# Expert tiles of a routed layer: bias rows of all experts kept in both weight buffers and picked by one-hot rows, the two additions of a tile issued together, eight output tiles

## The chip, the core and the metric

The kernel runs on one core of one Trainium2 chip. The metric is the device time of one execution in microseconds (us). Before the change it is 929.73 us, the median of 3 runs (926.41 to 929.73).

## What is computed

A four-layer network on 32 images and 32 texts (96 tokens of width 192 per batch): patch embedding with a binary activation, attention with 12 heads, a soft mixture of 64 slots, causal attention with rotary positions, and at the end a routed mixture of 8 experts. The change lies in the last one. Cut to what matters:

```
gate_logits = x_flat @ Wr                       # 3072 tokens, 8 experts
topw, topi = jax.lax.top_k(gate_logits, 2); topw = jax.nn.softmax(topw, axis=-1)
combine = zeros((T, 8)).at[arange(T)[:, None], topi].add(topw)
h = jax.nn.relu(jnp.einsum('td,edh->eth', x_flat, W1) + b1[:, None, :])    # 192 -> 768
y = jnp.einsum('eth,ehd->etd', h, W2) + b2[:, None, :]                     # 768 -> 192
out = jnp.einsum('te,etd->td', combine, y)                                 # added to the input
```

## The kernel before, in words

The program runs phase after phase on all engines. `route` sorts the (token, expert) pairs by expert into 31 tiles of 256 rows (`NTB`; 62 halves of 128 rows, `NTILES`), each tile with one expert. It leaves the row numbers (`g.idx`), the expert of each tile (`g.te`, and `g.te_less` in float), and in DRAM a table of the normalized tokens (`xtab`). It also splits the first bias `b1` into a high and a low part and writes both to a small DRAM table (`b1tab`, POOL, L1704 to L1711).

`expert_tiles` (L1840 to the end) then works the tiles off. Its stages are laid over each other: in step t the engines do the transposes of tile t, the first product of tile t-1, the second product of tile t-2, and bias, weight and addition of tile t-3. The order of the stages on an engine is written out by hand (`steps`, L94): steps 0 to 7 and the last ones are straight code, steps 8 to 27 are a loop of 4 steps per turn. All products run in split float32r (high and low part).

- **SP** (L1877 to L1892) loads for each tile the expert's first-layer weights into one of two buffers (`w_buf`) by four DMAs: three for the weights (L1881, L1883, L1885; 1344 KB) and one for the two bias rows from `b1tab` into rows 64 and 65 of part 3 (L1887, 6 KB). It waits until the first product of the tile two before is done. Behind the ones of tile 1 it loads the second bias for all experts (`x_b`, L1892).
- **POOL** fetches the rows of a tile by two indirect DMAs of 128 rows (L1900, into `late`) and adds the finished rows to the output by two indirect DMAs with addition (L1919). The loop over half tiles alternates: fetch of half t, addition of half t-10 (`BEHIND`). The additions of a tile wait until both additions of the tile before have landed, as two of them may hit the same output row. Behind its second fetch POOL writes the rows of ones that the bias rows are multiplied by (L1904 to L1907).
- **PE**: `first(k)`, k = 0 to 5 (L2037), five matmuls into one of three banks of PSUM; the last has 66 rows, 64 of the input's low part and the two of ones. It waits for DVE's low part of `first(k-3)`, since the bank comes free with it. `second(k)` (L2053, L2056) multiplies with the second weights, which all stay in SBUF. The transposes (L2019) stand between `second(1)` and `first(2)`.
- **ACT**: relu into the high part (L1936); `x_copy` takes the transposed input's high part (L1929) as soon as the transposes are done; `weigh` multiplies the output rows by the gate (L1943). Order in a step: relu 0, relu 1, x_copy, weigh 0, relu 2, weigh 1, relu 3 to 5.
- **DVE**: low parts of relu (L1976) and of the input (`x_rest`, L1969, L1970), the gate weights (`pick`, L1962, L1965), and `add_bias` (L1982 to L1990): it loads the expert's number from SBUF into a register (L1982, TENSOR_LOAD), waits for the second product and for `s_add` (the output tile must be free), and adds bias and product into one of four output tiles (`ys`, `NYS`; two tiles' worth). Order: add_bias 0, low parts 0 and 1, pick, x_rest, add_bias 1, low parts 2 to 5.

Of the kernel before, what the change touches and what calls it, by code (L numbers as in the profile page):

```python
# [146 lines left out]
def build(nc, A):  # L147
    with ExitStack() as ctx:
# [11 lines left out]
        g.te_less = sb("te_less", [128, NTB])  # L160
        g.te = sb("te", [128, NTB], mybir.dt.int32)
# [27 lines left out]
        with ExitStack() as lists:  # L189
# [32 lines left out]
            g.iota, g.padrow = small("iota", [128, 128]), small("padrow", [128, 2])  # L222
# [46 lines left out]
def expert_weights(nc, g, held):  # L269
# [27 lines left out]
    for i in range(NWB):  # L297
        g.w1_buf.append(halves(f"buf_{i}", [128, 4, F])[:, :, :])

# [986 lines left out]
def attention1(nc, A, g):  # L1286


    with ExitStack() as ctx:
# [8 lines left out]
        vv = sb("vv", [T, 4, D])  # L1298
        ra = sb("ra", [T, 2, 2 * D])
        rb = sb("rb", [T, 2, 2 * D])  # L1300
        qkT = sb("qkT", [HALF, 2, 4, T])
# [336 lines left out]
def route(nc, A, g):  # L1638


    with ExitStack() as ctx:  # L1641
# [26 lines left out]
        tokens = sb("tokens", [T, 2, PART, 128], F32R)  # L1668
        NL = NTILES + NTILES % 2
        occ = sb("occ", [T, 2, PART, NL], F32R)  # L1670
# [12 lines left out]
        def _(sp):  # L1683
# [16 lines left out]
            sp.wait_ge(g.s_b1r, 32)  # L1700
# [28 lines left out]
        def _(v):  # L1729
# [80 lines left out]
            v.tensor_scalar(g.te_less[:, :], tef[:, :], float(-NE), None, ALU.add)  # L1810
            v.wait_ge(s_list, 1)
# [23 lines left out]
def expert_tiles(nc, A, g):  # L1835
# [3 lines left out]
    with ExitStack() as ctx:  # L1839
# [3 lines left out]
        def sb(name, shape, dt=F32):  # L1843
# [3 lines left out]
        NYS = 4  # L1847
        BEHIND = 10
        xg, ys = carve(g.late, ([128, NX, DX], [128, NYS, D]))
        one = sb("one", [128, 256])  # L1850
        x_hi = sb("x_hi", [128, 2, 2, MT], F32R)
        x_lo = sb("x_lo", [128, 2, 2, MT], F32R)
        h_hi = sb("h_hi", [128, FC, MT], F32R)
        h_lo = sb("h_lo", [128, FC, MT], F32R)
        b2 = sb("b2", [128, NE, D])
        picked = sb("picked", [128, 2, 2])
        s_pick, s_cw = sem("pick"), sem("cw")
        (s_b2, s_mem, s_one, s_lo_v, s_sum, s_xTp, s_xh, s_xl, s_h1, s_hh, s_hl, s_y, s_ya, s_ys) = (
            sem(n) for n in ("b2", "mem", "one", "lo_v", "sum", "xTp", "xh", "xl", "h1", "hh", "hl", "y", "ya", "ys"))
# [11 lines left out]
        def _(sp):  # L1871
# [3 lines left out]
            sp.wait_ge(g.s_b1r, 32)  # L1875
            for i in range(NTB):
# [10 lines left out]
                sp.dma_start(buf[64:66, 3, :], A["b1tab"][:, bass.ds(e * F, F)]).then_inc(done, 16)  # L1887
# [7 lines left out]
        def _(pool):  # L1895
            for t in range(NTILES + BEHIND):
                if t < NTILES:
                    if t >= NX:
                        pool.wait_ge(s_cw, (t - NX) // 2 + 1)
                    pool.indirect_dma_start(out=xg[:, t % NX, :], out_offset=None, in_=A["xtab"][:, :],  # L1900
                                            in_offset=bass.IndirectOffsetOnAxis(ap=g.idx[:, t:t + 1], axis=0)
                                            ).then_inc(s_x[t % NX], 16)
                if t == 1:
                    pool.memset(one[:, :], 1.0).then_inc(s_mem, 1)  # L1904
                    pool.wait_ge(s_mem, 1)
                    for n in range(2):
                        pool.tensor_copy(x_lo[:, n, 1, :], one[:, :]).then_inc(s_one, 1)  # L1907
                        pool.wait_ge(s_one, n + 1)
                if t == NX - 1:
# [4 lines left out]
                i = t - BEHIND  # L1914
                if i >= 0:
                    pool.wait_ge(s_ys, i + 1)
                    if i >= 2:
                        pool.wait_ge(s_add, 32 * (i // 2))
                    pool.indirect_dma_start(out=A["out"][:, :],  # L1919
                                            out_offset=bass.IndirectOffsetOnAxis(ap=g.idx[:, i:i + 1], axis=0),  # L1920
                                            in_=ys[:, i % NYS, :], in_offset=None, compute_op=ALU.add).then_inc(s_add, 16)
# [3 lines left out]
        def _(act):  # L1925
            def x_copy(i, u):
                item(act, s_xTp, i)
                reused(act, s_h1, i, 2, FC)
                act.activation(x_hi[:, u % 2, :, :], b_x, ACT.Copy).then_inc(s_xh, 1)  # L1929
# [9 lines left out]
            def weigh(half):  # L1939
                def stage(i, u):  # L1940
                    act.wait_ge(s_ya, i * 2 + half + 1)
                    out = ys[:, (2 * u + half) % NYS, :]
                    act.activation(out, out, ACT.Copy, scale=g.cw[:, bass.ds(i * 2 + half, 1)]).then_inc(s_ys, 1)  # L1943
                return stage

            steps(act, NTB, [(relu(0), 1), (relu(1), 1), (x_copy, 0), (weigh(0), 3), (relu(2), 1), (weigh(1), 3),
# [3 lines left out]
        def _(v):  # L1950
# [5 lines left out]
            v.wait_ge(s_one, 2)  # L1956
# [23 lines left out]
            def add_bias(half):  # L1980
                def stage(i, u):
                    e = v.value_load(g.te[0:1, bass.ds(i, 1)], min_val=0, max_val=NE - 1)  # L1982
                    item(v, s_y, i, FC)
                    if not isinstance(i, int) or i >= 2:
                        v.wait_ge(s_add, i * 32 - 32)
                    out, bank = ys[:, (2 * u + half) % NYS, :], b_y[u % 2][half]
# [10 lines left out]
        def _(pe):  # L1997
            pe.wait_ge(s_one, 2)
# [24 lines left out]
            def first(k):  # L2023
                def stage(i, u):
                    w = g.w1_buf[u % NWB]
                    cols = slice(128 * k, 128 * k + 128)
                    if k == 0:
                        item(pe, s_xl, i)
                        if isinstance(i, int):
                            pe.wait_ge(g.s_w1[i % NWB], 64 * (i // NWB + 1))  # L2030
                        else:
                            pe.wait_ge(g.s_w1[u % NWB], (i - u) * (64 // NWB) + (64 * (u // NWB) + 64))
# [109 lines left out]
```

## Time and profile before

| | |
|---|---|
| median of 3 runs | 929.73 us |
| the profiled execution | 929.62 us |
| its span, first to last instruction | 927.8 us |
| PE busy over the span | 758.7 us (82%) |
| DVE, ACT, POOL busy | 540.8, 421.0, 354.6 us |
| expert tiles, first matmul to the span's end | from 657.5 us on |
| granted TensorE clock, mean | 0.886 |

Engines in the profile: PE is TensorE's matmuls, PEld its weight loads, DVE VectorE, ACT ScalarE, POOL GpSimd, SPq the queue of SyncE; a small q behind a name stands for that engine's sequencer. A matmul's busy time overlaps with the next one's, so PE's busy share says little; starts are what to read. Rows of the timeline give start, duration, engine, line, instruction, what it writes and reads, and in brackets the engine's idle time before it and what ended that.

### The profile page before, as it was taken

The page shows a single profiled execution, that of the slowest core. Times are in us where ns is not written, and L with a number is a line of the kernel's source. Part 1 is how long each engine was busy: PE and PEld are TensorE (multiplying, and loading weights), DVE is VectorE, ACT ScalarE, POOL GpSimd, SP SyncE. Part 2 cuts the span into 40 slices and gives each one's busy share as a digit, 9 for nine tenths or more (in the row PEclk, how much of TensorE's full clock was granted, in tenths as well). Part 3 has the DMA queues.
Part 4 walks back from the last instruction along what each step waited for, and adds up shares of the span by engine and source line. Part 5 has one row for each costly group of instructions (what it writes and reads, how often), then busy time and mean ns, then how long its engine had stood idle before and what let it go on. Part 6 is the DMA issues. An engine that isn't in the chain of part 4 may idle for free. (4 is left out here: it accounts for less than half of the span.)

```text
span 927.8 us, 23887 instructions
## 1 busy us (share of the span) xinstructions
PE 758.7 (82%) x8516; PEld 646.9 (70%) x8517; DVE 540.8 (58%) x1494; ACT 421.0 (45%) x1072; POOL 354.6 (38%) x391
## 2 busy tenths in 40 slices
PE   3689999999977766656689999926299999999992
PEld 3578888888864445434557778716299999999992
DVE  1698888787851311212467777779255555655562
ACT  3666776766642311111115777562144444444441
POOL 1433444444321000000103878410636666666654
PEclk9799999999965987787759999955599999999997
DMA  9419100000025999999347000062578888887872
GB/s 243 128 28 431 56 2 2 2 2 3 1 73 191 390 427 427 426 426 418 95 164 319 26 28 1 27 151 35 188 229 233 238 235 237 233 234 228 236 189 30
DMA packets 55133, 163.12 MB, mean 176 GB/s; under 512 B 12352, under 2 KB 30338, under 8 KB 50688
## 3 DMA queue, kind: packets, MB, share of 16 engines
q1 hardware_dynamic: 43072, 147.45, 43.1%
q0 software_dynamic: 11968, 14.41, 8.8%
q8 instruction: 62, 1.02, 0.4%
q14 instruction: 31, 0.25, 0.1%
HBM read 107.01 MB, written 12.16 MB: 128 GB/s over the span
## 5 line engine op out<-in xcount | busy, mean ns | idle before, releaser
L2037 PE MATMUL psum<-x_x_hi,w_buf 128*128 128x256 f32 x558 | 127.9, 299 | 14.1 <-DVE x_x_lo L1970 9.1
L1919 POOL DMA_INDIRECT out_h<-late,idx x62 | 98.4, 1587 | 71.4 <-DMA out_h<-late,idx 59.6
L2053 PE MATMUL psum<-w_pairs,x_h_hi 128*128 x372 | 116.1, 350 | 0.0
L1936 ACT ACTIVATE x_h_hi<-psum 128x256 fp32r<-128x256 f32 x186 | 68.5, 380 | 93.2 <-PE psum L2056 78.9
L2037 PEld LDWEIGHTS psum<-x_x_hi,w_buf 128*128 128x128 f32 x558 | 92.0, 192 | 20.5 <-DVE x_h_lo L1976 10.8
L1976 DVE SCALAR_TENSOR_TENSOR x_h_lo<-psum,x_h_hi 128x256 fp32r<-128x256 f32 x186 | 75.8, 420 | 52.3 <-ACT x_h_hi L1936 51.5
L2037 PE MATMUL psum<-x_x_lo,w_buf 128*128 128x256 f32 x372 | 97.5, 284 | 0.0
L2056 PE MATMUL psum<-w_pairs,x_h_lo 128*128 x372 | 93.2, 251 | 0.0
L1900 POOL DMA_INDIRECT late<-xtab,idx x62 | 61.2, 987 | 73.6 <-POOLq L1641 40.5
L536 POOL TENSOR_SCALAR a_u<-flat,a_mv 96x192 f32<-96x192 f32 x32 | 24.3, 758 | 133.8 <-DVE a_mv L708 133.8
L2056 PEld LDWEIGHTS psum<-w_pairs,x_h_lo 128*128 128x128 f32 x372 | 71.2, 191 | 0.0
L2037 PEld LDWEIGHTS psum<-x_x_lo,w_buf 128*128 128x128 f32 x372 | 71.1, 191 | 0.0
L2053 PEld LDWEIGHTS psum<-w_pairs,x_h_hi 128*128 128x128 f32 x372 | 70.4, 189 | 0.0
L639 ACT ACTIVATE ring<-psum 96x384 f32<-96x384 f32 x96 | 46.5, 484 | 28.2 <-PE psum L954 27.1
L1265 PE MATMUL psum<-flat,late 128*32 128x96 f32 x1152 | 35.8, 292 | 26.8 <-DMA flat<-in_slot_w 18.4
L1181 POOL MEMSET f_hid<- 96x96 f32 x1 | 0.2, 179 | 149.4 <-PE psum L1249 149.4
L1265 PEld LDWEIGHTS psum<-flat,late 128*32 128x32 f32 x1152 | 32.3, 134 | 33.6 <-DMA flat<-in_slot_w 23.2
L954 PE MATMUL psum<-ident,ring 96*96 96x96 f32 x384 | 50.4, 255 | 2.5 <-ACT ring L632 1.2
L1943 ACT ACTIVATE late<-late,cw 128x192 f32<-128x192 f32 x62 | 28.0, 452 | 51.1 <-DVE late L1990 51.1
L1207 DVE TENSOR_TENSOR m_y<-psum,m_y 128x384 f32<-128x384 f32 x8 | 7.3, 914 | 75.1 <-PE psum L1265 75.1
L1165 ACT ACTIVATE late<-late 128x512 f32<-128x512 f32 x24 | 14.7, 630 | 77.1 <-DVE late L1197 76.9
L1579 PE MATMUL psum<-late,b_xT 96*96 96x384 f32 x128 | 49.3, 510 | 0.0
(268 smaller groups left out, 1947.8 us busy)
## 6 DMA issues: line engine op xcount, KB each, us to landing
flat<-in_slot_w SPq DMA_DIRECT2D x23, 2304.0 KB, 30.3
w_buf<-w_first SPq DMA_DIRECT2D x31, 768.0 KB
ring<-in_slot_w SPq DMA_DIRECT2D x8, 2304.0 KB, 30.3
w_buf<-w_hi_a SPq DMA_DIRECT2D x31, 384.0 KB
flat<-in_moe_w SPq DMA_DIRECT2D x1, 10752.0 KB, 29.7
flat<-in_x_patches SPq DMA_DIRECT2D x4, 1536.0 KB, 14.5
w_buf<-w_first SPq DMA_DIRECT2D x31, 192.0 KB
flat<-in_slot_w SPq DMA_DIRECT2D x4, 576.0 KB, 33.8
```

Source lines behind the costliest of these rows:

```text
L639: act.activation(pT[:, r, :, :], bank_pT(b, r).rearrange("p (h t) -> p h t", t=T), ACT.Copy).then_inc(s_pTs, 1)
L954: mm = pe.transpose(bank_pT(b, r)[:, j * T:(j + 1) * T], p[:, b % 2, r * HG + j, :], g.ident[0:T, 0:T])
L1265: mm = pe.matmul(b_y[32 * quad:32 * quad + 32, 2 * r + j, :], hT[:, FC * r + k, B * c:B * (c + 1)], w2[:, c, k, half * HALF:(half + 1) * H ...
L1579: mm = pe.matmul(b_qk, xT[:, i % 2, k, :], wqkv[:, k, 0:2 * D], start=(k == 0), stop=(k == 1))
L1900: pool.indirect_dma_start(out=xg[:, t % NX, :], out_offset=None, in_=A["xtab"][:, :], in_offset=bass.IndirectOffsetOnAxis(ap=g.idx[:, t:t ...
L1919: pool.indirect_dma_start(out=A["out"][:, :], out_offset=bass.IndirectOffsetOnAxis(ap=g.idx[:, i:i + 1], axis=0), in_=ys[:, i % NYS, :], i ...
L1936: act.activation(h_hi[:, k, :], b_f[k % NF1], ACT.Relu).then_inc(s_hh, 1)
L1943: act.activation(out, out, ACT.Copy, scale=g.cw[:, bass.ds(i * 2 + half, 1)]).then_inc(s_ys, 1)
L1976: v.scalar_tensor_tensor(h_lo[:, k, :], b_f[k % NF1], 0.0, h_hi[:, k, :].bitcast(F32), ALU.max, ALU.subtract).then_inc(s_hl, 1)
L2037: mm = pe.matmul(b_f[k % NF1], w[0:rows, part, cols], x[0:rows, u % 2, c, :], start=(m == 0), stop=(m == len(terms) - 1))
L2053: pe.matmul(bank, h_hi[:, k, part], g.w_pairs[:, :, k, bass.ds(e, 1), :].rearrange("p two a d -> p two (a d)"), start=(k == 0), stop=False)
L2056: mm = pe.matmul(bank[:, 1, :], h_lo[:, k, part], g.w_pairs[:, 1, k, bass.ds(e, 1), :].rearrange("p a d -> p (a d)"), start=False, stop=(k ...
```

## The change

1. **Bias rows.** `route` writes the high and low bias rows of all 8 experts once into both weight buffers (rows 64 to 79 of part 3: four DMAs instead of two, on POOL). The DMA per tile and `b1tab` go. Instead of rows of ones, rows 64 to 79 of the input's low part hold a one in the two rows of the tile's expert: ACT writes them for each tile, ahead of the copy of the high part (16x256, from a column of ones times the one-hot column `g.te_hot`, which DVE computes once in `route`). The last matmul of `first(k)` has 80 rows instead of 66.
2. **Additions.** POOL issues both additions of tile t-5, then both fetches of tile t. Only the first of the two waits for the tile before.
3. **Output tiles.** Eight instead of four (four tiles' worth); DVE waits for the additions of the tile four before, where it waited for those of the tile two before.
4. **Memory.** `h_hi` and `h_lo` share a region (`w_work`) with tiles of the phases before, as do `x_one` and `x_picked` with `late`; the memory so freed holds the new output tiles (`x_ys`).

```diff
 (build)
+        g.te_hot = sb("te_hot", [128, NTB])
 (route, GpSimd)
             for i, row in enumerate((b1_hi, b1_lo)):
-                pool.dma_start(A["b1tab"][i:i + 1, :].rearrange("a (p f) -> (a p) f", p=128),
-                               row[:, :].bitcast(F32)).then_inc(g.s_b1r, 16)
+                for buf in g.w1_buf:
+                    to = buf[64 + NE * i:64 + NE * (i + 1), 3, :].bitcast(F32)
+                    pool.dma_start(to.rearrange("e (q f) -> e q f", q=16), row[:, :].bitcast(F32)).then_inc(g.s_b1r, 16)
 (route, VectorE)
+            v.tensor_scalar(g.te_hot[:, :], tef[:, :], padrow[:, 2:3], None, ALU.is_equal)
 (expert_tiles)
-        NYS = 4
-        BEHIND = 10
+        NYS = 8
+        BEHIND = 5
 (expert_tiles, SyncE, per tile)
-                sp.dma_start(buf[64:66, 3, :], A["b1tab"][:, bass.ds(e * F, F)]).then_inc(done, 16)
 (expert_tiles, GpSimd)
-            for t in range(NTILES + BEHIND):
...
+            def add_rows(t):
+                pool.wait_ge(s_add, 32 * t) if t else None
+                for i in (2 * t, 2 * t + 1):
+                    pool.wait_ge(s_ys, i + 1)
+                    pool.indirect_dma_start(out=A["out"][:, :],
...
+            for t in range(NTB + BEHIND):
+                if t >= BEHIND:
+                    add_rows(t - BEHIND)
+                if t < NTB:
+                    fetch(t)
 (expert_tiles, ScalarE, x_copy)
+                act.activation(x_lo[64:64 + 2 * NE, u % 2, 1, :], one[64:64 + 2 * NE, :].broadcast_to([2 * NE, MT]), ACT.Copy,
+                               scale=g.te_hot[64:64 + 2 * NE, bass.ds(i, 1)])
                 act.activation(x_hi[:, u % 2, :, :], b_x, ACT.Copy).then_inc(s_xh, 1)
 (expert_tiles, VectorE, add_bias)
-                    if not isinstance(i, int) or i >= 2:
-                        v.wait_ge(s_add, i * 32 - 32)
+                    if not isinstance(i, int) or i >= 4:
+                        v.wait_ge(s_add, i * 32 - 96)
 (expert_tiles, TensorE, first)
-                    terms = (..., (x_lo, 1, 3, 66))
+                    terms = (..., (x_lo, 1, 3, 64 + 2 * NE))
```

Where instructions move: POOL's queue at the head of `expert_tiles`, before the change (`late<-xtab` is a fetch, `out_h` an addition, `w_pairs` a part of the second weights):

```order
L1900 DMA late<-xtab,idx 128x260 x2
L1904 MEMSET x_one 128x256
L1907 CAST x_x_lo<-x_one 128x256 x2
L1900 DMA late<-xtab,idx 128x260 x2
L1913 TENSOR_TENSOR w_pairs<-flat,w_pairs 128x768 x4
L1900 DMA late<-xtab,idx 128x260 x7
L1919 DMA out_h<-late,idx 3328x192
L1900 DMA late<-xtab,idx 128x260
```

The same place after it:

```order
L1897 MEMSET late 128x1
L1903 DMA late<-xtab,idx 128x260 x4
L1924 TENSOR_TENSOR w_pairs<-flat,w_pairs 128x768 x4
L1903 DMA late<-xtab,idx 128x260 x6
L1911 DMA out_h<-late,idx 3328x192 x2
L1903 DMA late<-xtab,idx 128x260 x2
L1911 DMA out_h<-late,idx 3328x192 x2
L1903 DMA late<-xtab,idx 128x260 x2
L1911 DMA out_h<-x_ys,idx 3328x192 x2
```

The fetch that stood between the two additions of a tile now stands behind both, and the rows of ones are gone from between the fetches of tiles 0 and 1.

ACT's queue at the end of the loop over steps, before the change (two steps, from relu 0 and 1 on):

```order
L1936 ACTIVATE x_h_hi<-psum 128x256 x2
L1929 ACTIVATE x_x_hi<-psum 128x512
L1943 ACTIVATE late<-late,cw 128x192
L1936 ACTIVATE x_h_hi<-psum 128x256
L1943 ACTIVATE late<-late,cw 128x192
```

A step in the middle of the loop after it, with its register instructions:

```order
L1941 ACTIVATE w_work<-psum 128x256
L1938 REGISTER_ALU
L1940 REGISTER_ALU
L1941 ACTIVATE w_work<-psum 128x256
L87 REGISTER_ALU
L94 ISA
L1932 ISA
L1932 ACTIVATE x_x_lo<-late,te_hot 16x256
L1934 ACTIVATE x_x_hi<-psum 128x512
L1946 ISA
L1948 ISA
L1948 ACTIVATE x_ys<-x_ys,cw 128x192
```

The one-hot rows (L1932) stand between the wait for the transposes and the copy of the high part (before L1929, now L1934).

## Rows read from the trace of the kernel before

**Rows 1.** The page: the chain that ended last, by engine and line

```profile
DMA out_h<-late,idx 9%; PE psum L2037 4%; PE psum L2053 2%; POOL late L1900 2%; POOL out_h L1919 1%; PE psum L2056 1%; DMA late<-xtab,idx 1%; PE psum L2019 1%; DMA x_b<-in_moe_b 0%; SPq L1885 0%; DMA w_buf<-b1tab 0%; DVE x_h_lo L1976 0%; SPq L1881 0%; ACT late L1943 0%; SPq L1883 0%
```

**Rows 2.** Timeline, PE: transposes of tiles 3, 16, 17, 18, 29, 30

```profile
683.70 0.60 PE L2019 MATMUL psum<-ident,late 128*128 128x128 f32 x4
...
785.88 0.60 PE L2019 MATMUL psum<-ident,late 128*128 128x128 f32 x4
793.73 0.60 PE L2019 MATMUL psum<-ident,late 128*128 128x128 f32 x4
801.33 0.60 PE L2019 MATMUL psum<-ident,late 128*128 128x128 f32 x4
...
888.08 0.60 PE L2019 MATMUL psum<-ident,late 128*128 128x128 f32 x4
895.50 0.60 PE L2019 MATMUL psum<-ident,late 128*128 128x128 f32 x4
```

**Rows 3.** Timeline of step 17: ACT, DVE, and the matmul first(5)

```profile
794.45 0.60 ACT L1929 ACTIVATE x_x_hi<-psum 128x512 fp32r<-128x512 f32 x1
795.45 0.41 DVE L1970 TENSOR_TENSOR x_x_lo<-psum,x_x_hi 64x256 fp32r<-64x256 f32 x1
796.61 0.36 DVE L1987 TENSOR_TENSOR late<-psum,x_b 128x192 f32<-128x192 f32 x1 [0.75 <-DMA out_h<-late,idx]
797.75 0.50 PE L2037 MATMUL psum<-x_x_hi,w_buf 128*128 128x256 f32 x2
```

**Rows 4.** Register loads, L1982, steps 10, 17, 17: count, ns, start us

```profile
L1982 DVEq TENSOR_LOAD <-te x1: 425/425/425, 740.1 to 740.1; - x1
...
L1982 DVEq TENSOR_LOAD <-te x1: 301/301/301, 792.2 to 792.2; - x1
...
L1982 DVEq TENSOR_LOAD <-te x1: 957/957/957, 795.1 to 795.1; - x1
```

**Rows 5.** Timeline, POOL: additions and fetches at those loads

```profile
740.53 1.59 POOL L1919 DMA_INDIRECT out_h<-late,idx  x1 [0.30 <-ACT late L1943]
...
794.70 1.59 POOL L1919 DMA_INDIRECT out_h<-late,idx  x1 [0.30 <-issue]
796.60 0.98 POOL L1900 DMA_INDIRECT late<-xtab,idx  x1 [0.31 <-issue]
799.61 1.59 POOL L1919 DMA_INDIRECT out_h<-late,idx  x1 [2.02 <-DMA out_h<-late,idx]
```

**Rows 6.** Timeline, DVE: x_rest and add_bias 1 in step 16, a loop turn's first

```profile
788.15 0.41 DVE L1970 TENSOR_TENSOR x_x_lo<-psum,x_x_hi 64x256 fp32r<-64x256 f32 x1
789.01 0.36 DVE L1987 TENSOR_TENSOR late<-psum,x_b 128x192 f32<-128x192 f32 x1 [0.46 <-PE psum L2056]
```

**Rows 7.** Timeline, ACT: a weighting and the relu right behind it

```profile
876.57 0.46 ACT L1943 ACTIVATE late<-late,cw 128x192 f32<-128x192 f32 x1 [1.65 <-DVE late L1990]
876.93 0.64 ACT L1936 ACTIVATE x_h_hi<-psum 128x256 fp32r<-128x256 f32 x2
```

**Rows 8.** Timeline, PE: the one wait for a bias row, step 9

```profile
736.26 0.50 PE L2037 MATMUL psum<-x_x_hi,w_buf 128*128 128x256 f32 x2 [0.72 <-DMA w_buf<-b1tab]
```

**Rows 9.** Timeline, head of the tiles: SP's last two loads, DVE's wait

```profile
661.20 0.93 SPq L1887 DMA_DIRECT2D w_buf<-b1tab  x1
662.18 0.68 SPq L1892 DMA_DIRECT2D x_b<-in_moe_b  x1
666.65 0.22 DVE L1962 SCALAR_TENSOR_TENSOR x_picked<-late,te_less 128x4 f32<-128x4 f32 x1 [13.34 <-DMA x_b<-in_moe_b]
```

**Rows 10.** Timeline, tail: PE's last matmul and the last additions

```profile
910.91 0.25 PE L2056 MATMUL psum<-w_pairs,x_h_lo 128*128 x1
...
915.21 1.56 POOL L1919 DMA_INDIRECT out_h<-late,idx  x1 [0.30 <-issue]
919.45 1.55 POOL L1919 DMA_INDIRECT out_h<-late,idx  x1 [2.68 <-DMA out_h<-late,idx]
921.31 1.56 POOL L1919 DMA_INDIRECT out_h<-late,idx  x1 [0.31 <-issue]
```

More of the change, by code:

```diff
@@ L298, in expert_weights @@
         g.w1_buf.append(halves(f"buf_{i}", [128, 4, F])[:, :, :])
+    size = 2 * FC * MT
+    with nc.sbuf_tensor("w_early", [128, size], F32) as early:
+        g.work_early = early[:, :]
+    g.work = halves("work", [128, size])[:, :]
 def use_order():
@@ L1846, in expert_tiles @@
         NF1 = 3
[L1847 to L1850 removed]
+        NYS = 8
+        BEHIND = 5
+        xg, ys_early, picked, one = carve(g.late, ([128, NX, DX], [128, 4, D], [128, 2, 2], [128, 1]))
+        ys_late = sb("ys", [128, 4, D])
+        ys = [rows[:, i, :] for rows in (ys_early, ys_late) for i in range(4)]
         x_hi = sb("x_hi", [128, 2, 2, MT], F32R)
         x_lo = sb("x_lo", [128, 2, 2, MT], F32R)
[L1853 to L1854 removed]
+        h_hi, h_lo = carve(g.work, ([128, FC, MT], [128, FC, MT]))
         b2 = sb("b2", [128, NE, D])
[L1856 removed]
         s_pick, s_cw = sem("pick"), sem("cw")
[L1858 to L1859 removed]
+        (s_b2, s_one, s_lo_v, s_sum, s_xTp, s_xh, s_xl, s_h1, s_hh, s_hl, s_y, s_ya, s_ys) = (
+            sem(n) for n in ("b2", "one", "lo_v", "sum", "xTp", "xh", "xl", "h1", "hh", "hl", "y", "ya", "ys"))
         s_x, s_add = g.s_x, g.s_add
@@ L1895, in _, with fetch @@
         def _(pool):
-            for t in range(NTILES + BEHIND):
[L1897 to L1909, printed above, removed]
+            pool.memset(one[:, :], 1.0).then_inc(s_one, 1)
+            def fetch(t):
+                if t >= NX // 2:
+                    pool.wait_ge(s_cw, t - NX // 2 + 1)
+                for i in (2 * t, 2 * t + 1):
+                    pool.indirect_dma_start(out=xg[:, i % NX, :], out_offset=None, in_=A["xtab"][:, :],
+                                            in_offset=bass.IndirectOffsetOnAxis(ap=g.idx[:, i:i + 1], axis=0)
+                                            ).then_inc(s_x[i % NX], 16)
+            def add_rows(t):
+                pool.wait_ge(s_add, 32 * t) if t else None
+                for i in (2 * t, 2 * t + 1):
+                    pool.wait_ge(s_ys, i + 1)
+                    pool.indirect_dma_start(out=A["out"][:, :],
+                                            out_offset=bass.IndirectOffsetOnAxis(ap=g.idx[:, i:i + 1], axis=0),
+                                            in_=ys[i % NYS], in_offset=None, compute_op=ALU.add).then_inc(s_add, 16)
+            for t in range(NTB + BEHIND):
[3 more added lines that the diff above has]
+                    fetch(t)
+                if t == NX // 2 - 1:
                     for n in on_pool:
@@ L2129, in declare @@
     A["xtab"] = nc.dram_tensor("xtab", (NTOK + NPAD, DX), F32, kind="Internal").ap()
-    A["b1tab"] = nc.dram_tensor("b1tab", (2, NW1), F32, kind="Internal").ap()
     return A
```

38 lines of the change are left out of this document (13 added, 25 removed).

## The prediction

> **What bounds the kernel now.** Everything in question lies behind 657 us. I read four views, in this order. The page's chain of what ended last [rows 1] names the additions to the output (9% of the span) first. The reader is to see this and then distrust it: the chain follows the last instruction back, and POOL's additions, each waiting for the one before, make a chain of their own whether or not PE waits for them. So I went to the timeline, to what PE itself does. The transposes stand once in each step, so the distance between two of them is the period [rows 2]: tile 3 at 683.70, tile 30 at 895.50, 27 steps in 211.80 us, 7.84 each. The last of these steps took 7.42 us, and in it no matmul waits; that is PE's own work. 27 x 7.42 = 200.3 us, so **11.5 us of stalls** lie in these steps. Where: step 17 took 7.60 us [rows 2], and its one gap stands before first(5), the matmul at 797.75 [rows 3]. With T for the transposes' start that is T+4.02; without the 0.18 that the step is too long it would be T+3.84.
>
> What it waits for is a chain [rows 3]: ACT takes the input's high part at T+0.72, DVE ends x_rest at T+2.13, add_bias 1 begins at T+2.88, DVE's low part 2 follows it, and 1.14 behind add_bias 1 comes the matmul. Between x_rest and add_bias 1 lies a hole of 0.75 us that the row gives to the additions' DMA. It isn't theirs: add_bias 0 of the same tile waited for the same count and was past it. The hole is the load of the expert's number into a register [rows 4]. In step 17 one such load takes 0.30 us (792.2, for add_bias 0) and the next 0.96 (795.1, for add_bias 1). In step 10 the latter took 0.43, and there POOL's next DMA came 0.4 us behind the load's start (740.1 and 740.53); in step 17 POOL had begun an addition 0.4 us ahead of it [rows 4, 5]. The mean hole follows from the stalls: less 0.7 for a late bias row [rows 8] and my estimate of 1.1 for four loop turns, 9.7 / 27 = 0.36 a step; a stall is the hole plus 2.13 + 1.14 - 3.84, so the mean hole is 0.93.
>
> **The change, part by part.**
>
> *One-hot rows on ACT.* 31 instructions, each ahead of the high part's copy, on the very chain above. No row shows this shape. The nearest is weigh: 192 columns, the same kind of scale, 0.46 us, with the next instruction 0.36 behind its start [rows 7]. It has 64 columns more. ACT's copy of 512 columns takes 0.60 us [rows 3], two relus of 256 take 0.64 [rows 7], so a column costs at most 1.2 ns: 0.51 us, and it holds up the next instruction by **0.41**. Bounds: 0.36 and 0.51. x_rest then ends at T+2.54. If the load behind it takes 0.43, add_bias 1 begins at about T+2.8 and first(5) could go at T+3.9: next to no stall. If the hole stays, the 0.41 comes on top.
>
> What the load does then is the unknown. Low bound: stall 0. High bound: 0.36 + 0.41 = 0.77 a step. Between them the trace has an experiment of its own. In step 16, the first of a loop turn, x_rest ends at 788.56, T+2.68 with T = 785.88, 0.55 later than in step 17; add_bias 1 begins at T+3.13, only 0.25 later [rows 2, 6]. A later x_rest is half swallowed; with 0.41 instead of 0.55, add_bias 1 begins at T+3.07 and the stall is 0.37. And in the new order POOL's first addition follows weigh 0, which ends at about T+2.1 (0.72 + 0.41 + 0.60 + 0.46, less the overlap), so it comes 0.4 us behind the load's start at T+1.8, and POOL is idle before: the place it had in step 10. I take half of the steps as quick (0) and half as swallowed (0.37), because one row speaks for each: **0.2 us a step**. The loop turns stay. Sum for the 27 steps: 5.4 + 1.1 - 11.5 = **-5.0 us**.
>
> The Trainium skill speaks against this in "SBUF — State Buffer", section "SBUF: two separate sides": engine ports and DMA ports cannot contend with each other. By that rule loads wouldn't lengthen beside DMAs, and moving DMAs wouldn't shorten them; the sum would be by the high bound, the slower rival below. The trace shows the same load at 0.30 and 0.96 us three microseconds apart [rows 4], but no row says what lengthens it.
>
> *Additions together.* POOL's circle now: addition 1.59 + 0.3, the fetch between 0.98 + 0.3, then the second addition, whose landing is waited for: 794.70 to 799.61, 4.9 us [rows 5]. Together 8.1, about a step. Without the fetch between it is 6.8, or 6.1 with the tail's landing of 4.24 [rows 10]; the two fetches, 2.6 us, lie under the flight. PE's steps of 7.6 then set the pace and each pair waits for its rows. The fetches move later, to about T+6.3 and T+7.6, for transposes a step and more away. In the steps all this is worth nothing by itself where PE doesn't wait for additions; where it did, and DVE's wait for one of four output tiles ended last, it is in the 11.5. The same goes for *eight output tiles*.
>
> *Bias DMA.* SP issues three DMAs a tile instead of four. PE waited for that row once, 0.72 us [rows 8], also in the 11.5. Elsewhere the weights are in time with a period of 7.42, so they are with 7.6. If the freed DMA weren't the last of its group, this would be worth nothing. 80 rows instead of 66 in the matmul: nothing, it streams the same 256 columns.
>
> *Head.* The load of `x_b` is issued right behind the bias row's [rows 9], so it comes 0.98 earlier, and DVE's first pick and PE's start hang on its landing. POOL's small memset comes ahead of the first fetch, and two later fetches move up between the weights' traffic: **-0.5** (bounds -1.0 and +0.5). The four bias DMAs and te_hot in `route` lie beside other work: POOL has nothing else to do there, and DVE waits for PE's list behind te_less. Without that cover te_hot would cost some 0.2.
>
> *Tail.* PE ends at 911.16, yet the last two additions start at 919.45 and 921.31, 8.3 and 10.2 behind it [rows 10]. Now they keep up. Tile 29's second product ends 6 x 0.57 = 3.4 before PE's end; two low parts, bias and weight take 2.9, so its first addition goes at -0.5 and the second at +1.4. The landing takes 4.24 from there (915.21 to 919.45), so tile 30's go at 5.6 and 7.5: **-2.7** (bounds -2.0 and -4).
>
> Sum: -5.0 - 0.5 - 2.7 = -8.2 us. The profiled execution took 929.6 us, its span and 1.8 around it, and lies 0.1 below the median, so the forecast is **921.4 us**.
>
> **The rivals.**
>
> *The stalls go entirely* (0 a step: every load is a quick one, or the chain's word that additions set the pace is true after all). 1.1 - 11.5 = -10.4 in the steps: 916.0. For it: the quick load of step 10 has POOL's next DMA 0.4 behind, as all would now. Against it: it is one row, and a fetch in flight could be what matters.
>
> *Half swallowed everywhere* (0.37, as in step 16): -0.4 in the steps, 926.0. For it: only that row shows a later x_rest.
>
> *Slower: the one-hot rows lengthen the chain in full.* The hole stays at 0.93, stall 0.77 before every first(5): 27 x 0.77 + 1.1 - 11.5 = +10.4 in the steps, **936.8**. It decides from 0.50 a step on, where head and tail are used up (13.5 + 1.1 - 11.5 = 3.1). For it: the order on ACT is plain, and nothing shortens x_rest. Against it: [rows 6].
>
> *The additions don't keep up*, with both in flight together. A landing would have to take over 5.7 us instead of 4.2 to 4.9 to reach PE's 7.6. Then the tail's gain goes: 924.1, or more with new waits.
>
> **How the numbers follow.** A measurement of this kernel can tell about 0.5%, 4.6 us, from no change: under 925.1 is faster, over 934.4 slower. Chances: forecast (0.1 to 0.3 a step, 919 to 925) 0.45; stalls gone 0.14; half swallowed or additions late, around and above 925, 0.33; chain in full 0.08, of which 0.01 stays under 934.4. The first two are faster, 0.59; same 0.34; slower 0.07. The range from 916 to 931 leaves out the chain in full and the ends of the rest.
>
> **What would show it.** Right: 7.5 to 7.7 us between transposes; the one-hot instruction 0.5 us long and the high part's copy 0.4 later than T+0.72; holes before add_bias 1 of 0.2 to 0.6; first additions that start behind weigh 0 and no longer behind a landing; the last one about 7.5 us behind PE's end. Wrong: transposes 7.9 or more apart with first(5) behind DVE's low part 2; or register loads for add_bias 1 still about 1 us; or a new wait before first(0), for weights or for fetched rows.

## The result, and the profile after

The changed kernel takes **939.82 us**, the median of 4 runs (938.79 to 941.6), against 929.73 (926.41 to 930.45, 4 runs) before: a ratio of 1.0118, 95% interval 1.0089 to 1.0146. It is slower by 1.2%, about 11 us. The forecast was 921.4 with a range up to 931. The profiled execution took 939.68 us, with a span of 937.5, 9.7 more than the span before. Of kernels 6 and 10 below, one run and three runs lay over 1.5% above the fastest of their kernel; they are named there and stand outside the medians and ratios.

The page's chain of what ended last, and its line on the first matmul of a product:

```profile
PE 16%; DVE 4%; issue 3%; DMA 2%; DVEq 2%; ACT 2%; SPq 0%; POOL 0%; ACTq 0%; POOLq 0%
...
L2042 PE MATMUL psum<-x_x_hi,w_buf 128*128 128x256 f32 x558 | 128.7, 300 | 24.9 <-DVE w_work L1981 15.1
```

The additions' DMA, at 9% of the span in [rows 1], is gone from the head of this chain. What stands there now is the step's own loop: PE, DVE, ACT, and DVEq, the queue in which DVE's register loads run. PE sits 24.9 us before this matmul, most of it behind DVE's low parts (`w_work` L1981).

The timeline of PE, transposes of tiles 3, 16, 17 and 30, to be read against [rows 2]:

```profile
682.96 0.60 PE L2024 MATMUL psum<-ident,late 128*128 128x128 f32 x4
...
789.33 0.60 PE L2024 MATMUL psum<-ident,late 128*128 128x128 f32 x4
797.58 0.60 PE L2024 MATMUL psum<-ident,late 128*128 128x128 f32 x4
...
906.94 0.60 PE L2024 MATMUL psum<-ident,late 128*128 128x128 f32 x4
```

From tile 3 to tile 30 it is 223.98 us, 8.30 a step, where it was 211.80, 7.84 a step. PE's own work of 7.42 leaves a stall of 0.88 a step. So the 9.7 us of the span are: head -0.7 (682.96 against 683.70), these 27 steps +12.2, from tile 30's transposes to PE's last matmul +0.7, and the tail behind that -2.5.

Step 16, with T = 789.33 and 8.25 us long, in the timeline of ACT, DVE and PE, beside [rows 3]:

```profile
790.15 0.50 ACT L1932 ACTIVATE x_x_lo<-late,te_hot 16x256 fp32r<-16x256 f32 x1 [0.24 <-PE psum L2024]
790.66 0.60 ACT L1934 ACTIVATE x_x_hi<-psum 128x512 fp32r<-128x512 f32 x1
791.29 0.46 ACT L1948 ACTIVATE late<-late,cw 128x192 f32<-128x192 f32 x1
...
791.64 0.41 DVE L1975 TENSOR_TENSOR x_x_lo<-psum,x_x_hi 64x256 fp32r<-64x256 f32 x1
792.85 0.36 DVE L1992 TENSOR_TENSOR late<-psum,x_b 128x192 f32<-128x192 f32 x1 [0.81 <-PE psum L2061]
793.99 0.50 PE L2042 MATMUL psum<-x_x_hi,w_buf 128*128 128x256 f32 x2 [0.59 <-DVE w_work L1981]
```

Read it down. The one-hot rows begin at T+0.82, 0.10 later than the copy did. In the loop their column comes by a register, and the register instructions stand between ACT's wait and the activation. The copy begins at T+1.33, 0.51 behind the one-hot rows and 0.61 later than before. x_rest ends at T+2.72 (2.13 before). Then comes a hole of 0.80 to add_bias 1 at T+3.52, and 1.14 behind its start the matmul, at T+4.66 where PE wants it at T+3.84. The hole is there as before. Step 16 begins a turn of the loop; in step 17 x_rest ends at T+2.71 and the hole is 0.89, so it isn't the turn. Over the 27 steps the hole goes from 0.12 to 1.15 and is 0.80 on the mean. Before the change its mean over the same steps was 0.76.

The one-hot instructions, the load of this step, and all loads (count, ns min/median/max, first and last start):

```profile
L1932 ACT ACTIVATE x_x_lo<-late,te_hot x31: 501/502/505, 658.3 to 907.6; 16x256 fp32r<-16x256 f32 x31
...
L1987 DVEq TENSOR_LOAD <-te x1: 1037/1037/1037, 791.3 to 791.3; - x1
...
L1987 DVEq TENSOR_LOAD <-te x62: 300/580/1383, 681.3 to 924.1; - x62
```

The last one-hot row starts at 907.61, in the straight steps, where the column is a constant: 0.67 behind its transposes, where the copy stood 0.64 behind them before (888.72 and 888.08). So most of the 0.10 goes with the register. The load in step 16 starts at 791.3, takes 1.04 us, and add_bias 1 follows 0.5 behind its end. It is as long as the long one in [rows 4]. Over all steps from tile 3 on, the load for add_bias 1 takes 1.03 us on the mean, where it took 0.98 before.

POOL in the same step, beside [rows 5]:

```profile
792.55 1.62 POOL L1911 DMA_INDIRECT out_h<-late,idx  x1 [2.47 <-ACT late L1948]
794.48 1.58 POOL L1911 DMA_INDIRECT out_h<-late,idx  x1 [0.31 <-ACT late L1948]
796.37 1.01 POOL L1903 DMA_INDIRECT late<-xtab,idx  x1 [0.30 <-issue]
```

POOL does what was forecast. It is idle for 2.47 us, the first addition waits for weigh 0 (which ends at 791.75) and no longer for a landing, and it begins 1.2 behind the load's start, where 0.4 was forecast. By then the load, slow all the same, has ended (792.3).

Head and tail, beside [rows 9] and [rows 10]:

```profile
660.51 1.00 SPq L1893 DMA_DIRECT2D x_b<-in_moe_b  x1
665.73 0.22 DVE L1967 SCALAR_TENSOR_TENSOR late<-late,te_less 128x4 f32<-128x4 f32 x1 [13.26 <-DMA x_b<-in_moe_b]
...
923.08 0.25 PE L2061 MATMUL psum<-w_pairs,w_work 128*128 x1
928.93 1.55 POOL L1911 DMA_INDIRECT out_h<-x_ys,idx  x1 [2.25 <-DMA out_h<-late,idx]
930.79 1.56 POOL L1911 DMA_INDIRECT out_h<-x_ys,idx  x1 [0.30 <-issue]
```

The last two additions start 5.6 and 7.5 us behind PE's end (923.33), the two figures of the forecast.

### The profile page after: what moved, and what is told of

Its sections match the earlier page's. It is cut to its first block and busy times, and to the rows that moved or that the text cites. A ratio compares the mean times of both kernels' runs of the same rounds, so it can differ in the third digit from the quotient of the medians.

```text
span 937.5 us, 23842 instructions
## 1 busy us (share of the span) xinstructions
PE 758.5 (81%) x8516; PEld 645.5 (69%) x8517; DVE 543.0 (58%) x1495; ACT 435.9 (46%) x1103; POOL 356.3 (38%) x391
## 5 line engine op out<-in xcount | busy, mean ns | idle before, releaser
L2042 PE MATMUL psum<-x_x_hi,w_buf 128*128 128x256 f32 x558 | 128.7, 300 | 24.9 <-DVE w_work L1981 15.1
L2058 PE MATMUL psum<-w_pairs,w_work 128*128 x372 | 116.1, 350 | 0.0
L1941 ACT ACTIVATE w_work<-psum 128x256 fp32r<-128x256 f32 x186 | 67.3, 377 | 85.6 <-PE psum L2061 75.1
L1981 DVE SCALAR_TENSOR_TENSOR w_work<-psum,w_work 128x256 fp32r<-128x256 f32 x186 | 75.0, 419 | 50.1 <-ACT w_work L1941 49.4
L2061 PE MATMUL psum<-w_pairs,w_work 128*128 x372 | 93.1, 250 | 0.0
L2061 PEld LDWEIGHTS psum<-w_pairs,w_work 128*128 128x128 f32 x372 | 71.2, 192 | 0.0
L2058 PEld LDWEIGHTS psum<-w_pairs,w_work 128*128 128x128 f32 x372 | 70.4, 189 | 0.0
L1911 POOL DMA_INDIRECT out_h<-late,idx x32 | 51.1, 1596 | 46.9 <-ACT late L1948 34.7
L1911 POOL DMA_INDIRECT out_h<-x_ys,idx x30 | 47.8, 1594 | 39.7 <-ACT x_ys L1948 17.0
L1270 PE MATMUL psum<-flat,late 128*32 128x96 f32 x1152 | 34.7, 286 | 27.8 <-DMA flat<-in_slot_w 19.8
```

The source lines that it names most:

```text
L1270: mm = pe.matmul(b_y[32 * quad:32 * quad + 32, 2 * r + j, :], hT[:, FC * r + k, B * c:B * (c + 1)], w2[:, c, k, half * HALF:(half + 1) * H ...
L1911: pool.indirect_dma_start(out=A["out"][:, :], out_offset=bass.IndirectOffsetOnAxis(ap=g.idx[:, i:i + 1], axis=0), in_=ys[i % NYS], in_offs ...
L1941: act.activation(h_hi[:, k, :], b_f[k % NF1], ACT.Relu).then_inc(s_hh, 1)
L1981: v.scalar_tensor_tensor(h_lo[:, k, :], b_f[k % NF1], 0.0, h_hi[:, k, :].bitcast(F32), ALU.max, ALU.subtract).then_inc(s_hl, 1)
L2042: mm = pe.matmul(b_f[k % NF1], w[0:rows, part, cols], x[0:rows, u % 2, c, :], start=(m == 0), stop=(m == len(terms) - 1))
L2058: pe.matmul(bank, h_hi[:, k, part], g.w_pairs[:, :, k, bass.ds(e, 1), :].rearrange("p two a d -> p two (a d)"), start=(k == 0), stop=False)
```

## The experiments

"Kernel 3" below is the kernel of experiment 3, and so on. Two theories stand after this profile. **A**: the one-hot rows lengthen the chain transposes, copy, x_rest, add_bias 1 by 0.6 us a step, and that is the slowdown. **B**: the register load is made long by what the new order of the additions puts beside it. Below, the period is the distance from tile 3's to tile 30's transposes divided by 27, from one profile each; two profiles of one kernel (3 and 11) differ by 0.08 in it. With each group of runs the kernel before was timed again on the same chip: 928.31, 927.76 and 928.69 us.

**1. One-hot rows later.** The changed kernel, with the one-hot rows behind relu 2, off the chain.

```diff
-                act.activation(x_lo[64:64 + 2 * NE, u % 2, 1, :], ..., scale=g.te_hot[64:64 + 2 * NE, bass.ds(i, 1)])
                 act.activation(x_hi[:, u % 2, :, :], b_x, ACT.Copy).then_inc(s_xh, 1)
+            def hot(i, u):
+                reused(act, s_h1, i, 2, FC)
+                act.activation(x_lo[64:64 + 2 * NE, u % 2, 1, :], ..., scale=...).then_inc(s_hot, 1)
-            steps(act, NTB, [..., (relu(2), 1), (weigh(1), 3),
+            steps(act, NTB, [..., (relu(2), 1), (hot, 0), (weigh(1), 3),
+                        item(pe, s_hot, i)
```

> Theory A (the one-hot instruction stands in the chain transposes, high part, x_rest, register load, bias addition, low part 2, first(5), and each 0.6 us there goes through to PE): taken out of the chain, behind relu 2, it lies in a hole of ACT of 1.7 us and costs nothing; 28 steps x 0.6 = 17 us less than the changed kernel's 939.8, so 923, with 7.7 us between transposes. Rival B (the paired additions and fetches, or the bias rows in the weight buffers, slow the register loads and the transfers; the one-hot instruction is hidden): no change, 938 to 940, and 8.3 us between transposes.

Measured: 929.95 us (10 runs), ratio to before 1.0016 (1.0001 to 1.0031). Its timeline, transposes of tiles 3 and 30, and ACT in one step:

```profile
679.51 0.60 PE L2028 MATMUL psum<-ident,late 128*128 128x128 f32 x4
...
782.44 0.60 ACT L1933 ACTIVATE x_x_hi<-psum 128x512 fp32r<-128x512 f32 x1
...
783.92 0.50 ACT L1937 ACTIVATE x_x_lo<-late,te_hot 16x256 fp32r<-16x256 f32 x1
...
892.28 0.60 PE L2028 MATMUL psum<-ident,late 128*128 128x128 f32 x4
```

The period is 7.88, 0.42 less than in the changed kernel, and the slowdown of 10 us is gone. The expected gain over before does not come. The 0.6 of the chain isn't paid in every step: over the 27 steps x_rest ends 0.47 earlier on the mean than in the changed kernel (T+2.22 against T+2.68), and 0.42 of that comes back.

**2. The same instruction in the kernel before.** A 16x256 activation into scratch, ahead of the copy; nothing else changes.

```diff
+                act.activation(extra[64:64 + 2 * NE, :], one[64:64 + 2 * NE, 0:1].broadcast_to([2 * NE, MT]), ACT.Copy,
+                               scale=g.te_less[64:64 + 2 * NE, bass.ds(i, 1)])
                 act.activation(x_hi[:, u % 2, :, :], b_x, ACT.Copy).then_inc(s_xh, 1)
```

> The kernel before with one instruction more, of the one-hot rows' shape (16x256 from a column, scale from a column, into a scratch tile), ahead of the copy of the high part. Theory A: each step 0.5 to 0.6 us longer, 929.7 + 15 = 945. Rival B: within 2 us of 929.7. Between them, that a later x_rest is half swallowed by a shorter register load: 937.

Measured: 939.59 us (4 runs), ratio 1.0121 (1.0089 to 1.0153). Its timeline:

```profile
680.84 0.60 PE L2023 MATMUL psum<-ident,late 128*128 128x128 f32 x4
...
746.49 0.50 ACT L1930 ACTIVATE x_extra<-x_one,te_less 16x256 fp32r<-16x256 f32 x1 [0.24 <-PE psum L2023]
747.00 0.60 ACT L1932 ACTIVATE x_x_hi<-psum 128x512 fp32r<-128x512 f32 x1
...
902.17 0.60 PE L2023 MATMUL psum<-ident,late 128*128 128x128 f32 x4
```

Period 8.20. One instruction of 0.50 us, with the copy 0.51 behind it, makes the whole slowdown in a kernel that has none of the other parts. Its 27 steps are 9.5 us longer than before; in the changed kernel they are 12.2 longer, and its tail gives 2.5 back. Theory A holds, though not for 0.6 a step: 939.59 lies under the 945 expected by it. Here too x_rest ends 0.47 later on the mean than before, since in the first step of each loop turn it was late already (below).

**3. One register load a tile.** The changed kernel; add_bias 1 uses the register that add_bias 0 of the tile loaded.

```diff
-                    e = v.value_load(g.te[0:1, bass.ds(i, 1)], min_val=0, max_val=NE - 1)
+                    if half == 0:
+                        numbers_of[u] = v.value_load(g.te[0:1, bass.ds(i, 1)], min_val=0, max_val=NE - 1)
+                    e = numbers_of[u]
```

> The changed kernel with the expert's number loaded into a register once per tile instead of twice: add_bias 1 takes the register of add_bias 0. Theory A: the hole of 0.8 us between x_rest and add_bias 1 is that load; without it the stall before first(5) falls from 0.9 us to 0.1 or 0.2, 27 x 0.75 = 20 us less: 919.5, 7.55 us between transposes. If the hole is something else (a wait for the additions, the second product): 938 to 940.

Measured: 916.58 us (4 runs), ratio 0.9881 (0.9843 to 0.9919). Its timeline, transposes and, in one step, x_rest and add_bias 1:

```profile
679.97 0.60 PE L2028 MATMUL psum<-ident,late 128*128 128x128 f32 x4
...
787.89 0.41 DVE L1975 TENSOR_TENSOR x_x_lo<-psum,x_x_hi 64x256 fp32r<-64x256 f32 x1
788.22 0.34 DVE L1996 TENSOR_TENSOR x_ys<-psum,x_b 128x192 f32<-128x192 f32 x1
...
882.47 0.60 PE L2028 MATMUL psum<-ident,late 128*128 128x128 f32 x4
```

add_bias 1 now follows x_rest with no hole, and the period is 7.50. The longer chain is still there, but without the load it ends before PE wants its result. So the slowdown needs both, the one-hot rows and the load behind them. The last step of each turn of the loop takes 7.60 to 7.66 where its neighbours take 7.41 to 7.43: the four turns cost 0.8 us in all.

**4. The additions' part alone.** The changed kernel with the rows of ones, `b1tab` and the bias DMA of before; order of POOL and eight output tiles as changed.

```diff
+                sp.dma_start(buf[64:66, 3, :], A["b1tab"][:, bass.ds(e * F, F)]).then_inc(done, 16)
...
-                act.activation(x_lo[64:64 + 2 * NE, u % 2, 1, :], ..., scale=g.te_hot[64:64 + 2 * NE, bass.ds(i, 1)])
...
-                    terms = (..., (x_lo, 1, 3, 64 + 2 * NE))
+                    terms = (..., (x_lo, 1, 3, 66))
```

> The change without its bias part: rows of ones and one bias DMA a tile as before, but both additions of a tile together and eight output tiles. Theory A: the additions' part is worth 2.5 us in the tail and about 1 to 3 in steps 7 and 8: 925 to 926. Rival B (the new order of additions and fetches is what slows the steps): 935 or more.

Measured: 928.16 us (10 runs), ratio 0.9996 (0.9974 to 1.0018), period 7.81 (transposes at 686.24 and 897.03). That is over the 925 to 926 expected: the additions' part alone changes nothing that shows (the interval reaches from 2.4 us less to 1.7 more, and the tail's gain, 2.3 us in this profile, lies within it). With it in both, the bias part makes the changed kernel slower. POOL in one of its steps:

```profile
784.25 1.62 POOL L1909 DMA_INDIRECT out_h<-late,idx  x1 [1.15 <-DMA out_h<-x_ys,idx]
786.18 1.57 POOL L1909 DMA_INDIRECT out_h<-late,idx  x1 [0.30 <-issue]
...
792.16 1.62 POOL L1909 DMA_INDIRECT out_h<-late,idx  x1 [1.82 <-DMA out_h<-late,idx]
```

The circle, from one tile's first addition to the next tile's, is 7.91 us here: 1.93 from the first addition to the second, and 5.98 from there until the next tile's first may go. The first waits for a landing again, although the pair was put together.

**5. One-hot rows later and one load** (edits 1 and 3 together).

```diff
+            steps(act, NTB, [..., (relu(2), 1), (hot, 0), (weigh(1), 3),
...
+                    e = numbers_of[u]
```

> The changed kernel with both edits of the first two runs: the one-hot instruction behind relu 2, and one register load per tile. With one load alone 27 steps took 202.5 us, 7.50 each, which leaves 2.2 us over PE's own 7.42. Theory A (the chain to low part 2 is then off the path, with or without the one-hot rows in it): 915 to 917, within 1.5 us of the run with one load alone. If the one-hot rows still cost their 0.4 a step there: 906.

Measured: 921.44 us (7 runs), ratio 0.993 (0.9905 to 0.9955), period 7.54. That is over the 915 to 917 expected, and beside the 921.02 that kernel 3 takes when timed again (11). Where the one-hot rows stand makes no difference that shows once the load is out.

**6. One load in the kernel before** (the edit of 3 on the kernel before).

```diff
+                    if half == 0:
+                        numbers_of[u] = v.value_load(g.te[0:1, bass.ds(i, 1)], min_val=0, max_val=NE - 1)
+                    e = numbers_of[u]
```

> The kernel before with one register load per tile and nothing else. Theory A: its stalls, 7.84 less 7.42 a step, were that load's, so it drops to about 7.5 a step: 928.3 - 27 x 0.34 = 919, or 917 to 920. If the additions' circle of 8.1 us (with only two tiles of output rows behind it) then sets the pace, as the chain of what ended last suggests: 926 to 928, and DVE waits for the additions.

Measured: 932.04 us (8 runs, 926.82 to 939.64; one more took 947.21), ratio 1.0048 (1.0013 to 1.0082). A clear miss. Its period is 7.68, with one step of 10.84. Its waits between 690 and 900 us (us in total, times, longest), and the longest of them in the timeline:

```profile
POOL out_h L1919 <- DMA out_h<-late,idx: 47.8, 25, 4.5
...
DVE late L1991 <- DMA out_h<-late,idx: 19.8, 14, 3.5
```

```profile
839.72 0.36 DVE L1991 TENSOR_TENSOR late<-psum,x_b 128x192 f32<-128x192 f32 x1 [3.48 <-DMA out_h<-late,idx]
```

This is a real wait for one of the four output tiles, and DVE's low parts and PE queue behind it. add_bias 1 follows x_rest with no hole in every step, so the load is gone as in 3. But the additions' circle (7.75 on the mean of the tiles that wait for a landing) leaves no slack against a step of 7.5, a single landing of over 6 us makes it longer still, and DVE runs out of output tiles. [Rows 1] named the additions, and they are the next bound, though not what PE waited for in that kernel.

**7. No weight stream.** The changed kernel with only tiles 0 and 1 loaded; the other products take those weights.

```diff
-            for i in range(NTB):
+            for i in range(NWB):
```

> The changed kernel without the weight loads of tiles 2 to 30 (their products are computed with the weights of tiles 0 and 1). Theory W (the register load is slow while the weights stream in): all register loads 0.3 to 0.4 us, stall before first(5) 0.1 to 0.2, about 920. Rival P (POOL's indirect DMAs slow it): register loads of add_bias 1 still about 1 us, 937 to 940.

Measured: 917.29 us, one run, period 7.53. All its register loads:

```profile
L1987 DVEq TENSOR_LOAD <-te x62: 298/308/557, 680.3 to 901.7; - x62
```

**8. No additions.** The changed kernel without the additions of tiles 0 to 29; DVE waits for the weighting instead of the landing.

```diff
-                pool.wait_ge(s_add, 32 * t) if t else None
+                if t < NTB - 1:
+                    return
...
-                        v.wait_ge(s_add, i * 32 - 96)
+                        v.wait_ge(s_ys, i * 2 - 6)
```

> The changed kernel without the additions of tiles 0 to 29 (only the last tile's are made). Theory W: the register loads stay at about 1 us and the steps at 8.2 to 8.3 us; only the tail is shorter, by 4 to 6 us (tile 30's additions needn't wait for tile 29's): 934 to 936. Rival P: register loads 0.3 to 0.5, steps under 7.8, 920 to 925.

Measured: 925.49 us, one run, period 7.73. All its register loads:

```profile
L1988 DVEq TENSOR_LOAD <-te x62: 298/443/973, 684.0 to 911.0; - x62
```

Seen together, on the mean from tile 3 on: the load for add_bias 1 takes 1.03 us in the changed kernel, 0.51 without the additions (8), and 0.31 without the weight stream, though additions and fetches run on (7). Run 7 refutes rival P. Run 8 refutes theory W as it was expected there: the load did not stay at 1 us. So the weight stream lengthens the load, the additions lengthen it further beside that stream, and alone they don't. Theory B fails in what it says of the change: the load was as long with the old order (0.98 before) as it is in 4 (0.97) and in the changed kernel.

**9. The additions' part and one load** (edits 4 and 3 together).

```diff
+                    e = numbers_of[u]
```

> The additions' part of the change alone (rows of ones and one bias DMA a tile as before, no one-hot rows) with one register load per tile. What the bias part is worth once the chain is short. Theory A: first(5) has slack with and without the one-hot rows (0.6 against a hole of 0.8), so the same as the whole change with one load, 917 to 920, up to 2 us more for PE's waits on the late bias row. If the one-hot rows still cost: 905 to 910.

Measured: 920.17 us (6 runs), ratio 0.9907 (0.9889 to 0.9926), period 7.53.

**10. Old order on POOL.** Kernel 3, with fetches and additions alternating as before and eight output tiles kept.

```diff
-            for t in range(NTB + BEHIND):
-                if t >= BEHIND:
-                    add_rows(t - BEHIND)
-                if t < NTB:
-                    fetch(t)
+            for t in range(NTILES + 2 * BEHIND):
+                if t < NTILES:
...
+                i = t - 2 * BEHIND
+                if i >= 0:
+                    pool.wait_ge(s_ys, i + 1)
+                    if i >= 2:
+                        pool.wait_ge(s_add, 32 * (i // 2))
```

> The changed kernel with one register load and eight output tiles, but POOL's queue as before: addition, fetch, addition, fetch. If pairing shortens the additions' circle (theory C, as the prediction had it: 6.8 against 8.1 us): the additions fall behind PE's 7.5 by 0.6 a tile, 18 us over 31 tiles, some of it is swallowed by the four tiles of slack, some comes back as waits of DVE and a longer tail, 925 or more. If the circle is the same both ways (theory D: two additions in flight together land in 5.3 to 6.3 us, one alone in 4.2 to 4.9, and 3.2 + 4.6 is 1.9 + 5.8): within 2 us of the paired kernel, 917 to 920.

Measured: 926.44 us (9 runs, 924.67 to 934.83; three more took 938.58, 942.86 and 943.63), ratio 0.9989 (0.9963 to 1.0014), period 7.72. Most of what it has over kernel 3 stands in two steps, of 11.47 and 9.98 us. Its timeline before the first of these:

```profile
753.94 1.59 POOL L1916 DMA_INDIRECT out_h<-late,idx  x1 [3.72 <-DMA out_h<-x_ys,idx]
755.83 0.98 POOL L1903 DMA_INDIRECT late<-xtab,idx  x1 [0.30 <-issue]
...
761.49 1.09 PE L2022 MATMUL psum<-ident,late 128*128 128x128 f32 x4 [3.90 <-issue]
```

POOL waits 3.72 us for a landing with fetches queued behind. The fetch at 755.83 brings the second half of tile 13's rows, and PE, ready for that tile's transposes at 757.59, waits 3.90. The profile puts PE's wait down to "issue"; that it is for these rows is my reading of POOL's order. The circle is 7.71 us on the mean, against 7.41 and 7.57 in the two profiles of the paired kernel (3 and 11): close to theory D, but the time isn't. So what pairing is worth here lies less in a shorter circle than in the fetches, which no longer stand behind the wait for a landing.

**11. Kernel 3 again**, unchanged, beside 9 and 10.

```diff
 (no difference to 3)
```

> The changed kernel with one register load per tile once more, beside the two others on the same chip and with more rounds, since a program's phases before 657 us vary by 3 us from run to run: 916 to 920, 1.2% under the kernel before.

Measured: 921.02 us (6 runs), ratio 0.9918 (0.9892 to 0.9944), period 7.58. The two timings of kernel 3 differ by 4.4 us, but both intervals lie below 1. Kernel 9 has the same time as this one: with one load, the bias part makes no difference that shows.

The ratios in one table (7 and 8, which leave out part of the work, have none):

| kernel | bias part | additions' part | loads a tile | ratio to before |
|---|---|---|---|---|
| changed | yes | yes | 2 | 1.0118 |
| 1 | yes, one-hot rows later | yes | 2 | 1.0016 |
| 2 | instruction only | no | 2 | 1.0121 |
| 4 | no | yes | 2 | 0.9996 |
| 6 | no | no | 1 | 1.0048 |
| 10 | yes | output tiles only | 1 | 0.9989 |
| 9 | no | yes | 1 | 0.9907 |
| 5 | yes, one-hot rows later | yes | 1 | 0.993 |
| 3, again as 11 | yes | yes | 1 | 0.9881, 0.9918 |

## Why the prediction was wrong, point by point

**The step that failed** is the stall: "half of the steps as quick (0) and half as swallowed (0.37) ...: 0.2 us a step". With the loop turns it was to be 0.24, and it measured 0.88. Both premises fell: the register load behind x_rest became no quicker (0.98 us before, 1.03 after), and so nothing swallowed what the one-hot rows add to the chain. The rival "the one-hot rows lengthen the chain in full" is what happened, 936.8 forecast and 939.82 measured; it had 0.08. That its number came so near is partly luck: it took the hole too long (0.93, measured 0.80) and the one-hot rows' delay too short (0.41, measured 0.61).

*Quick loads.* They come in a few steps, no more than before. Kernel 2 keeps the old order of the additions and is as slow as the changed kernel. I had taken one short load (425 ns in step 10) and the POOL instruction behind it [rows 4, 5] as a pattern. By 7 and 8 it is the weight stream that lengthens the load, and the additions beside it, and the weight stream runs in every step. No placing of POOL's instructions takes that stream away.

*Swallowed.* Next to nothing. The prediction's mean hole of 0.93 was worked back from the stalls; read off the timeline step by step it was 0.76 before, and is 0.80 after. x_rest ends at T+2.22 on the mean before and at T+2.68 after, 0.47 later, and the stall grew by 0.45. Taking the instruction off the chain gave back 0.42 a step (1), adding it cost 0.35 (9.5 us over 27 steps, 2), and x_rest moved by 0.47 both times. That it isn't 0.6 has its cause in what [rows 6] showed and the prediction misread: in the first step of the turns at tiles 12, 16, 20 and 24, x_rest ended at T+2.68 to T+2.73 already before the change, and it ends at T+2.71 or T+2.72 there after it (tile 16: 788.56 - 785.88 in [rows 6], 792.05 - 789.33 in the rows of step 16 above). The one-hot rows delay it in the other steps only. The shorter hole of such a first step (0.62 on the mean of five before, 0.65 after) goes with the step's place in the turn, not with a later x_rest: in the other loop steps x_rest moved from T+2.13 to T+2.71 and the hole went from 0.83 to 0.93.

*The size of the instruction.* Its duration was right, 0.51 forecast and 0.50 measured. How long it holds up the copy was not: 0.51, the high bound, where I took 0.41 from a weighting and a relu that overlap. It is 0.51 in the straight steps too (899.56 to 900.07), where no register is involved. And 0.10 for the register's handling was missing, though the order of ACT's queue showed it. Together 0.61 instead of 0.41.

*Additions together.* Worth nothing by itself (4), as forecast. But the circle was forecast at 6.8 or 6.1, and on the mean of the pairs that wait for a landing it measures 7.4 to 7.6 (3, 4, 9 and 11; 1.93 + 5.5 or 5.6). From the second addition's start to the next tile's first it takes 5.5 to 5.6 us in a pair, where it took 4.75 with a fetch between. That is the condition "a landing would have to take over 5.7" of the rival on additions, nearly reached. Once the steps are fast it is the part that counts: 9 against 6, which differ in the order and in the output tiles, is -1.4%, and 10 against 11, with eight output tiles in both, puts 0.7% of it down to the order.

*Bias DMA, output tiles, 80 rows.* Nothing that shows with two loads, as forecast, and for the DMA and the 80 rows none with one load either (9 beside 11). The output tiles are worth something with one load: DVE waits 19.8 us for landings with four (6), 2.7 with eight and POOL's order as before (10), and the ratio is 0.6% lower, with intervals that just touch. No run has them as its only change.

*The loop turns.* The 1.1 us put down for them in the sum had no row behind it; kernel 3 shows 0.8.

*Head and tail.* -0.5 forecast and -0.7 found; -2.7 forecast. Behind PE's end it is -2.5, but the steps behind tile 30's transposes have the same stall, +0.7. The first transposes of all start anywhere from 653.7 to 660.5 us in the profiles of these kernels, so the head's figure is not shown by one pair of profiles.

*The rule weighed.* The register load takes 0.31, 0.51 and 1.03 us on the mean with only DMA traffic taken away around it (7, 8 and the profile after). The Trainium skill, "SBUF — State Buffer", section "SBUF: two separate sides", says that engine ports and DMA ports cannot contend. For the time of this register load the measurement decides against what I drew from it, yet the sum came out near the one by that rule, because the load was as long before the change as after it (0.98 and 1.03). "DMA: Bandwidth & Descriptors" in the Trainium skill, section "Latency and other measured facts", gives a floor of about 600 ns for a `tensor_load`, without saying from which memory; the loads here, from SBUF, take 0.30 us at the least.

*Open.* By which path DMA traffic slows a register load, and why the copy doesn't overlap with the one-hot instruction as a relu does with a weighting: no run tried these. The later landing of a pair is settled in part. In the last pairs, with no fetch or weight load beside them, it is 3.6 to 3.8 us, and without the weight stream (7) only two of the 30 pairs wait for a landing at all, where all 30 do in kernel 3. So the two additions alone don't make it late; it takes the weight stream beside them. Why a pair suffers more from the stream than two additions with a fetch between is not shown.

The best version is the changed kernel with one register load a tile: 916.58 and 921.02 us, about 1% under before. Kernel 9, without the bias part, does as well as the second of these.

## What to carry over

Before putting work ahead of a stage, find the whole chain from it to the bound engine's wait and its slack: here it was already late by about 0.4 us a step, so what was added to it was paid in full, step after step. An attribution names the last semaphore, not always the cause: the hole was put down to additions [rows 3], then to PE, and was a register load that removing one line took away. After removing a stall, look for what has just under the same period (here the additions, about 7.7 us against a step of 7.84 with the stall and 7.5 without), since a fix can be worth nothing without the part that frees the next bound.

## What was unexpected of the hardware

- A register load from SBUF on DVE's queue took, on the mean, 0.31 us beside indirect additions and fetches without the weight stream, 0.51 beside stream and fetches without the additions, 1.03 beside all three, and at most 1.38 in the profile after (1.74 in the one before). The instruction that follows it began 0.5 us behind its end.
- A 16x256 activation with a column as its scale takes 0.50 us, and the next activation starts 0.51 behind its start: no overlap, where a relu started 0.36 behind the start of a weighting of 0.46 [rows 7].
- Two indirect additions of 128 rows issued 1.93 us apart, beside the weight stream: 5.5 to 5.6 us on the mean from the second's start to the start of what waits for both, 4.75 with a fetch between them; 3.6 to 3.8 in the tail, where nothing else is under way.
